# Two copies of a convolution's input and accumulator, and a new order of ScalarE's work

## The chip, the cores and the metric

The kernel runs on one core of a Trainium2 chip. The metric is the device time of one execution in microseconds (us), lower being better.

## What is computed

`x` is 8 samples of 256 tokens by 256 channels. A first layer (attention with modulated weights) adds to `x`; a second layer, a gated state-space block, adds to the result. The change lies in the first third of the second layer, cut here to what matters:

```python
xr, gate = jnp.split(x @ W_in.T, 2, axis=-1)          # 256 -> 512 + 512 channels
xr = xr + t_emb[:, None, :]
xc = conv1d(xr, W_conv, taps=4, causal, per channel) + b_conv
xc = silu(xc)
mu, var = xc.mean(-1), xc.var(-1)                     # layer norm over the 512 channels
xn = (xc - mu) / sqrt(var + 1e-5) * ln_g + ln_b
Bm, Cm, dt = split(xn @ W_xproj.T, 3)                 # 16 numbers each per token
...
_, ys = scan(step, h0, (Ad, Bd, xn, Cm))              # 256 steps in time, all samples at once
y = ys + D * xn
return y * silu(gate) @ W_out.T
```

## The kernel before, in words

The program is written out by hand, one instruction stream for each engine, with semaphores between them; within an engine the order of the code is the order of the work. There are four stages: the first layer, sample by sample (0 to 301 us of the trace); the **convolution stage**, sample by sample (301 to 385 us); a stage that normalises the rows, splits them into three bf16 parts and writes them to DRAM (385 to 464 us); the scan of 256 steps with the output projection (464 to 719 us). The stages follow one another: the statistics at L1266 to L1271 need all eight samples of the convolution stage, and everything later needs the statistics.

Samples are b = 0 to 7, channels lie on the 128 partitions in CT = 4 groups of 128. For each sample the convolution stage has these steps:

- TensorE, `project_in(b)` (L868 to L880): 8 column blocks, each of two matmuls of 256 columns. The first four blocks go to banks 4 and 5 (the convolution's input, signalled by `xr_done`), the other four to banks 6 and 7 (the gate, signalled by `gate_done`). The first half waits until ScalarE has emptied banks 4 and 5 of the sample before (`xr_in`), the second half until it has emptied banks 6 and 7 (`gate_out`). Each fp32 matmul has two records in the profile, so one sample's half is x16 and the whole is x32.
- ScalarE, `take_projection` (L569 to L587): four activations take banks 4 and 5 into the padded input `xrp` (L575), four multiply it by the last tap into the accumulator `acc` (L580, then `tap3_ready`), two take the gate through SiLU into `gateT` (L585) after a wait for `gate_done`.
- VectorE, `convolve` (L1234 to L1242): twelve multiply-adds put the other three taps onto `acc` (then `conv_done`).
- ScalarE, `gate_conv` (L596 to L601): SiLU of `acc` into `xcT` (then `xcT_ready`). `xcT` has one copy, before and after the change.
- TensorE, `to_tokens` (L912 to L928): waits for `xcT_ready`, turns `xcT` into token order with 8 transposes (L919, into banks 0 and 1), then multiplies it with the small weights `wxg` (L926, 48 columns each, into bank 2; then `xcT_used`).
- ScalarE, `take_tokens` (L589 to L594): two copies of banks 0 and 1 into `xc`.
- VectorE, `take_raw` (L1244 to L1253): a copy of bank 2 and two batch-norm statistics instructions.

The order on each engine before the change, for b from 1 to 7:

- ScalarE: `take_projection(b)`, `take_tokens(b-1)`, `gate_conv(b)`. `take_projection(b)` waits until the convolution of b-1 is done (L573), since `xrp` and `acc` have one copy each.
- VectorE: `convolve` of b, `take_raw(b-1)`.
- TensorE (L907 to L935): `project_in(b)`, `to_tokens(b-1)`, beginning with `project_in(0)` and `project_in(1)`; at the end `to_tokens(6)` and `to_tokens(7)` follow each other. In the loop a turn is thus the pair "project in b, then to tokens b-1":

```python
with pe.Fori(2, B) as b:
    project_in(b, False)
    to_tokens(b - 1, False)
to_tokens(B - 1, False)
```

GpSimd clears the three padding columns of `xrp` once (L397) and otherwise fills constants; SyncE issues no transfer in this stage.

Of the kernel before, what the change touches and what calls it, by code (L numbers as in the profile page):

```python
# [19 lines left out]
ALU = mybir.AluOpType  # L20
ACT = mybir.ActivationFunctionType
AX = mybir.AxisListType

P = 128
B, S, H = 8, 256, 256
NH, HD = 16, 16
C, NS = 512, 16
TAPS = 4
HALVES = S // P
NT = B * HALVES  # L30
HT, CT = H // P, C // P
# [50 lines left out]
def build(nc, x_tok, xT, s1_row, condT, w5T, winT, wconv, bconv, ln_row, lnT, wxT, wxdt, wdtT, bdt_row, alog_row,  # L82
          woT, ident_d, mask8_d, out):
    with ExitStack() as ctx:
        def sb(name, shape, dt=F32):
            return ctx.enter_context(nc.sbuf_tensor(name, shape, dt))

        def sem(name):
            return ctx.enter_context(nc.semaphore(name))
# [7 lines left out]
        bank = [ctx.enter_context(nc.psum_tensor(f"bank{i}", [P, 512], F32)) for i in range(8)]  # L97
# [7 lines left out]
        wcv = sb("wcv", [P, CT, TAPS])  # L105
# [92 lines left out]
        def sbc(name, shape, dt=F32):  # L198
            return conv_bufs.enter_context(nc.sbuf_tensor(name, shape, dt))

        xrp = sbc("xrp", [P, CT, TAPS - 1 + S])
        acc = sbc("acc", [P, CT, S])
        xcT = sbc("xcT", [P, CT, S])
        conv_bufs.close()
        xpart = sb1("xpart", [P, HALVES * XS, 3, C], BF16)
# [21 lines left out]
        s = {n: sem(n) for n in names}  # L227
# [5 lines left out]
        def _(sp):  # L233
# [76 lines left out]
            def store_b(t):  # L310

                for j, (_, bp) in enumerate(PAIRS):
                    rows = bd_d[j * BD_J:j * BD_J + B * (S * P + NS)].rearrange("(b q) -> b q", b=B)[:, 0:S * P]
                    rows = rows.rearrange("b (t c) -> t b c", c=P)[:, :, 0:NS]
                    sp.dma_start(rows[t * P:(t + 1) * P], bpart[:, bp, t, :].rearrange("p (b d) -> p b d", b=B))\
                      .then_inc(s[f"bd_out{t}"], 16)
# [58 lines left out]
        def _(pool):  # L375
            own = Own(pool, s["pool_own"])
# [17 lines left out]
                        .then_inc(s["part_ready"], 1)  # L394

            pool.wait_ge(s["x1_ready"], B)
            nc.gpsimd.memset(xrp[:, :, 0:TAPS - 1], 0.0).then_inc(s["const_pool"], 1)  # L397
            nc.gpsimd.memset(xst[:, :, :, :], 1.0)
            nc.gpsimd.memset(bst[:, :, :, :], 0.0)
            nc.gpsimd.memset(cst[:, :, :, :], 0.0)  # L400
# [9 lines left out]
            with pool.Fori(0, B // XS) as i:  # L410
                for k in range(XS):
                    b = i * XS + k
# [60 lines left out]
        def _(act):  # L473
# [92 lines left out]
            act.wait_ge(s["x1_ready"], B)  # L566
            nc.scalar.activation(tA[:, :], tA[:, :], ACT.Tanh).then_inc(s["dt_out"], 1)

            def take_projection(b, first):  # L569

                act.wait_ge(s["xr_done"], b * 2 + 2)
                if not first:
                    act.wait_ge(s["conv_done"], b)  # L573
                for c in range(CT):
                    ins = nc.scalar.activation(xrp[:, c, TAPS - 1:], bank[4 + c // 2][:, (c % 2) * S:(c % 2 + 1) * S],  # L575
                                               ACT.Identity, bias=cond[:, c, bass.ds(b, 1)])
                ins.then_inc(s["xr_in"], 1)
                act.wait_ge(s["xr_in"], b + 1)
                for c in range(CT):
                    ins = nc.scalar.activation(acc[:, c, :], xrp[:, c, TAPS - 1:], ACT.Identity,  # L580
                                               bias=bcv[:, c:c + 1], scale=wcv[:, c, TAPS - 1:TAPS])
                ins.then_inc(s["tap3_ready"], 1)
                act.wait_ge(s["gate_done"], b * 2 + 2)
                for c2 in range(2):
                    ins = nc.scalar.activation(gateT[:, 2 * c2:2 * c2 + 2, bass.ds(b * S, S)],  # L585
                                               bank[6 + c2][:, :].rearrange("p (k s) -> p k s", k=2), ACT.Silu)
                ins.then_inc(s["gate_out"], 1)  # L587

            def take_tokens(b):  # L589

                for t in range(HALVES):
                    act.wait_ge(s["tok_ready"], b * HALVES + (t + 1))
                    nc.scalar.activation(xc[:, b * HALVES + t, :], bank[t][:, :], ACT.Copy)\
                        .then_inc(s["tok_taken"], 1)  # L594

            def gate_conv(b, first):  # L596

                act.wait_ge(s["conv_done"], b + 1)
                if not first:
                    act.wait_ge(s["xcT_used"], b)  # L600
                nc.scalar.activation(xcT[:, :, :], acc[:, :, :], ACT.Silu).then_inc(s["xcT_ready"], 1)  # L601

            take_projection(0, True)
            gate_conv(0, True)
            with act.Fori(1, B) as b:
                take_projection(b, False)
                take_tokens(b - 1)
                gate_conv(b, False)
            take_tokens(B - 1)
            act.wait_ge(s["rt_in"], 5)  # L610
            nc.scalar.activation(rt[:, :], var_e[:, :], ACT.Sqrt).then_inc(s["rt_out"], 1)
# [459 lines left out]
        def _(dve):  # L1071
            v = nc.vector
            own = Own(dve, s["vec_own"])
# [147 lines left out]
            for c in range(CT):  # L1221
                v.tensor_scalar(wxg[:, c, :], wx[:, c, :], lnt[:, 0, c:c + 1], None, ALU.mult)
                ins = v.tensor_scalar(lnb_rep[:, c, :], ones[:, :], lnt[:, 1, c:c + 1], None, ALU.mult)
# [7 lines left out]
            sample(B - 1, False, True, False)  # L1231
            add_l0(B - 1)

            def convolve():  # L1234
                for k in range(TAPS - 1):
                    for c in range(CT):
                        ins = v.scalar_tensor_tensor(acc[:, c, :], xrp[:, c, k:k + S], wcv[:, c, k:k + 1],  # L1237
                                                     acc[:, c, :], ALU.mult, ALU.add)
                    if k < TAPS - 2:
                        own.mark(ins)  # L1240
                        own.settle()
                ins.then_inc(s["conv_done"], 1)  # L1242

            def take_raw(b):  # L1244

                dve.wait_ge(s["tok_taken"], b * HALVES + HALVES)
                dve.wait_ge(s["xcT_used"], b + 1)
                v.tensor_copy(raw[:, bass.ds(b * HALVES, HALVES), :],
                              bank[2][:, 0:2 * 64].rearrange("p (t n) -> p t n", t=HALVES)[:, :, 0:NP3])\
                    .then_inc(s["raw_ready"], 1)  # L1250
                for t in range(HALVES):
                    ins = v.bn_stats(bn[:, b * HALVES + t, :], xc[:, b * HALVES + t, :])
                own.mark(ins)  # L1253

            dve.wait_ge(s["tap3_ready"], 1)
            convolve()
            with dve.Fori(1, B) as b:
                own.enter(b - 1, TAPS - 1)
                dve.wait_ge(s["tap3_ready"], b + 1)
                convolve()  # L1260
                take_raw(b - 1)
            own.leave(B - 1)
            take_raw(B - 1)
            own.settle()
            for n in range(NT):
# [181 lines left out]
```

## Time and profile before

| | us |
|---|---|
| median of three runs | 718.82 |
| lowest and highest of them | 718.27 and 719.84 |
| span of the profiled execution (first to last instruction) | 718.9 |
| convolution stage, from the first `xrp` activation to the last copy of bank 2 | 301.4 to 385.2 |

Busy shares over the whole span: TensorE 72%, VectorE 70%, ScalarE 37%, GpSimd 18%. The page gives no time for the profiled execution beside its span, so the span stands for both. In the rows below, times are microseconds from the start of the span; a row of a timeline merges neighbouring instructions of one line (x12 is twelve of them), and what stands in square brackets is the time that the engine was idle before the row and the instruction that released it. PEclk is the clock that TensorE was granted, as a part of full speed: 1.00 is 2.4 GHz and 0.50 is 1.2 GHz. A matmul's record ends when the result is there, so matmuls that follow closely overlap in their records.

### The profile page before, as it was taken

Reading aid. Unit: us, or ns where it says so; the run is one execution under the profiler, and the core shown is the slowest. Engines: PE = TensorE matmul, PEld = TensorE weight load, DVE = VectorE, ACT = ScalarE, POOL = GpSimd, SP = SyncE. Lnnn points to the kernel's source line nnn. Section 1 sums busy time; section 2 is a strip of 40 time slices with the busy share of each in tenths; the row PEclk is TensorE's granted clock in tenths of the full one; section 3 lists DMA queues with packets and bytes.
Section 4 is the critical chain, followed back from the end, with each engine's and each line's share of the span. In section 5 each row is a group of like instructions: output and inputs, shape, how many; then the busy total and the mean of one; then the engine's idle time right before and its main releaser. Section 6 shows DMA issues by size and latency. Waiting matters only on the chain.

```text
span 718.9 us, 10868 instructions
## 1 busy us (share of the span) xinstructions
PE 515.4 (72%) x3248; PEld 302.7 (42%) x3264; DVE 500.2 (70%) x820; ACT 263.7 (37%) x513; POOL 129.9 (18%) x136
## 2 busy tenths in 40 slices
PE   3667888888888878999972100187677668888878
PEld 2555556465564634688862000011111113333357
DVE  2834858667595775467666897188898878888832
ACT  2314453445545433366673555012112112222211
POOL 5302012020120200240000246011221112222100
PEclk9868999999999998999995555589999989999999
DMA  9635161624606240040000234644454446556341
GB/s 356 216 71 103 31 129 26 113 52 80 118 16 130 51 81 1 1 175 0 0 0 1 88 117 157 77 90 86 98 98 93 92 85 128 117 115 135 84 147 51
DMA packets 44889, 64.88 MB, mean 90 GB/s; under 512 B 19536, under 2 KB 34256, under 8 KB 41152
## 3 DMA queue, kind: packets, MB, share of 16 engines
q1 hardware_dynamic: 41520, 59.26, 37.0%
q0 software_dynamic: 784, 3.15, 1.1%
q10 hardware_dynamic: 2560, 2.16, 0.9%
q8 instruction: 12, 0.20, 0.1%
q14 instruction: 13, 0.11, 0.0%
HBM read 41.88 MB, written 22.61 MB: 90 GB/s over the span
## 4 chain that ended last, share of the span: by engine, by line
PE 37%; issue 20%; DVE 19%; DMA 10%; ACT 7%; POOL 4%; SPq 2%; ACTq 0%; DVEq 0%; POOLq 0%
DVE zst L1378 15%; PE bank L718 6%; PE bank L965 6%; ACT ex L540 5%; PE bank L975 5%; PE bank L736 4%; DMA bst<-bd_d 3%; DMA qst<-mT 3%; PE bank L746 3%; PE bank L1061 2%; PE bank L773 2%; PE bank L727 2%; PE bank L756 2%; POOL xpart L416 2%; DVE mx L1175 2%
## 5 line engine op out<-in xcount | busy, mean ns | idle before, releaser
L1378 DVE CUSTOM_DVE_ANT_0 zst<-zst,bank,hi 128x512 f32<-128x512 f32 x256 | 191.3, 747 | 43.6 <-PE bank L965 22.2
L965 PE MATMUL bank<-xst,bst 128*128 128x512 bf16 x240 | 87.5, 404 | 102.5 <-DMA bst<-bd_d 57.7
L648 ACT ACTIVATE yb<-bank,ybias 128x512 f32<-128x512 f32 x64 | 44.1, 689 | 186.9 <-PE bank L975 182.4
L965 PEld LDWEIGHTS bank<-xst,bst 128*128 128x128 bf16 x256 | 24.7, 98 | 187.3 <-DVE zst L1378 120.5
L1175 DVE TENSOR_REDUCE mx<-bank 128x2 f32<-128x512 f32 x128 | 80.0, 686 | 18.1 <-PE bank L736 17.0
L540 ACT ACTIVATE ex<-bank 128x512 f32<-128x512 f32 x128 | 66.1, 609 | 41.1 <-PE bank L746 23.5
L975 PE MATMUL bank<-zst,cst 128*32 128x512 f32 x512 | 70.2, 621 | 0.9 <-DVE zst L1378 0.9
L1193 DVE TENSOR_TENSOR esum<-ex 128x1024 f32<-128x1024 f32 x32 | 39.1, 1223 | 42.7 <-ACT ex L540 42.7
L1237 DVE SCALAR_TENSOR_TENSOR acc<-xrp,wcv,acc 128x256 f32<-128x256 f32 x96 | 40.1, 481 | 29.4 <-ACT acc L580 28.8
L877 PE MATMUL bank<-xres,win 128*128 (+1 forms) x256 | 57.6, 382 | 1.2 <-ACT gateT L585 0.7
L718 PE MATMUL bank<-xnT,w 128*128 128x256 f32 x192 | 52.3, 422 | 5.1 <-ACT xnT L487 5.1
L389 POOL TENSOR_TENSOR qk<-qk,part 128x512 f32<-128x512 f32 x16 | 19.7, 1233 | 196.8 <-ACT part L502 196.7
L877 PEld LDWEIGHTS bank<-xres,win 128*128 128x128 f32 x256 | 47.9, 190 | 8.5 <-issue 1.2
L746 PE MATMUL bank<-qst,kst 97*128 97x256 bf16 x256 | 40.5, 280 | 13.0 <-DMA qst<-mT 10.2
L736 PE MATMUL bank<-kst,qst 96*128 96x256 bf16 x256 | 38.6, 286 | 8.0 <-DMA kst<-qk_d 4.8
L718 PEld LDWEIGHTS bank<-xnT,w 128*128 128x128 f32 x192 | 38.7, 212 | 12.5 <-ACT xnT L487 6.9
L416 POOL TENSOR_TENSOR xpart<-xrem,xpart 128x512 bf16<-128x512 f32 x16 | 20.7, 1311 | 109.6 <-ACT xpart L627 109.6
L423 POOL TENSOR_TENSOR cst<-cP,mask 128x64 f32<-128x64 f32 x32 | 9.6, 302 | 163.3 <-PE bank L975 163.3
L763 PE MATMUL bank<-ex,vp 128*32 128x256 f32 x512 | 33.9, 382 | 7.2 <-ACT ex L540 7.2
L746 PEld LDWEIGHTS bank<-qst,kst 97*128 97x128 bf16 x256 | 20.0, 99 | 36.2 <-ACT ex L540 20.1
L736 PEld LDWEIGHTS bank<-kst,qst 96*128 96x128 bf16 x256 | 24.1, 101 | 22.1 <-issue 8.2
L1154 DVE SCALAR_TENSOR_TENSOR xres<-bank,dc,xres 128x256 f32 (+1 forms) x32 | 14.0, 480 | 22.8 <-PE bank L781 21.9
(169 smaller groups left out, 712.3 us busy)
## 6 DMA issues: line engine op xcount, KB each, us to landing
qk_d<-part SPq DMA_DIRECT2D x64, 96.0 KB, 2.5
xs_d<-xpart SPq DMA_DIRECT2D x16, 384.0 KB, 2.6
xst<-xs_d SPq DMA_DIRECT2D x32, 192.0 KB
xst<-xs_d SPq DMA_DIRECT2D x32, 128.0 KB
y_d<-yb SPq DMA_DIRECT2D x128, 32.0 KB
ytk<-y_d SPq DMA_DIRECT2D x16, 256.0 KB, 3.6
bst<-bd_d SPq DMA_DIRECT2D x32, 102.0 KB
qst<-qk_d SPq DMA_DIRECT2D x8, 384.0 KB, 4.6
```

Of the source, the lines that this page charges most:

```text
L540: nc.scalar.activation(ex[:, g % 2, n % 4, :], bank[4 + n % 4][:, :], ACT.Exp, scale=SCALE)\
L648: nc.scalar.activation(yb[:, par, g, :], bank[4 + n % 2][:, :], ACT.Identity, bias=ybias[:, bass.ds(i * (2 * CH // 4) + n, 1)]).then_inc(s ...
L718: ins = mm(bank[bk][:, o * S:(o + 1) * S], w5[:, w, k, o * P:(o + 1) * P], xnT[:, k, :], start=k == 0, stop=k == HT - 1)
L736: ins = mm(bank[4 + n % 4][:, t * S:(t + 1) * S], qst[0:96, par, HEADS[n], t * P:(t + 1) * P], kst[0:96, par, HEADS[n], :], start=True, st ...
L746: ins = mm(bank[4 + n % 4][:, t * S:(t + 1) * S], kst[0:97, par, HEADS[n], t * P:(t + 1) * P], qst[0:97, par, HEADS[n], :], start=True, st ...
L877: ins = mm(bank[4 + c // 2][:, (c % 2) * S:(c % 2 + 1) * S], win[:, k, c * P:(c + 1) * P], xres[:, k, bass.ds(b * S, S)], start=k == 0, st ...
L965: mm(bank[k][:, :], bst[:, par, step, :], xst[:, par, step, :], start=True, stop=True)\
L975: ins = mm(bank[4 + g % 2][32 * k:32 * k + 32, :], cst[:, par, step, :], zst[:, step % ZR, :], start=True, stop=True)
L1175: v.tensor_reduce(mx[:, :, HEADS[n]:HEADS[n] + 1], bank[4 + n % 4][:, :].rearrange("p (t k) -> p t k", t=HALVES), AX.X, ALU.max)\
L1193: v.tensor_tensor(esum[:, g % 2, :, :], ex[:, g % 2, :, 0:S], ex[:, g % 2, :, S:], ALU.add)\
L1237: ins = v.scalar_tensor_tensor(acc[:, c, :], xrp[:, c, k:k + S], wcv[:, c, k:k + 1], acc[:, c, :], ALU.mult, ALU.add)
L1378: v._custom_dve(bass.dve_ops.TENSOR_ADD_SAT, out=zst[:, t % ZR, :], in0=zst[:, (t - 1) % ZR, :], in1=bank[t % 4][:, :], s0=hi[:, t:t + 1], ...
```

## The change

`xrp` and `acc` get a second copy each, used in turn by even and odd samples; the memset clears the padding of both. ScalarE's order becomes: `take_projection(0)`, `take_projection(1)`, `gate_conv(0)`, then for b = 0 to 5 `take_tokens(b)`, `take_projection(b+2)`, `gate_conv(b+1)`, and at the end `take_tokens(6)`, `gate_conv(7)`, `take_tokens(7)`. `take_projection(b)` now waits for the convolution of b-2, and for its own SiLU of b-2 ahead of the accumulator. VectorE's order of work is as before, its loop covers two samples. TensorE's code is not touched. The new buffers lie where `xpart` has its place later, so no other buffer moves.

```diff
-        xrp = sbc("xrp", [P, CT, TAPS - 1 + S])
-        acc = sbc("acc", [P, CT, S])
+        xrp = sbc("xrp", [P, 2, CT, TAPS - 1 + S])
+        acc = sbc("acc", [P, 2, CT, S])
...
-            nc.gpsimd.memset(xrp[:, :, 0:TAPS - 1], 0.0).then_inc(s["const_pool"], 1)
+            nc.gpsimd.memset(xrp[:, :, :, 0:TAPS - 1], 0.0).then_inc(s["const_pool"], 1)
...
-            def take_projection(b, first):
+            def take_projection(b, k):
 
                 act.wait_ge(s["xr_done"], b * 2 + 2)
-                if not first:
-                    act.wait_ge(s["conv_done"], b)
+                if not (isinstance(b, int) and b < 2):
+                    act.wait_ge(s["conv_done"], b - 1)
                 for c in range(CT):
-                    ins = nc.scalar.activation(xrp[:, c, TAPS - 1:], bank[4 + c // 2][:, (c % 2) * S:(c % 2 + 1) * S],
+                    ins = nc.scalar.activation(xrp[:, k, c, TAPS - 1:], bank[4 + c // 2][:, (c % 2) * S:(c % 2 + 1) * S],
                                                ACT.Identity, bias=cond[:, c, bass.ds(b, 1)])
                 ins.then_inc(s["xr_in"], 1)
                 act.wait_ge(s["xr_in"], b + 1)
+                if not (isinstance(b, int) and b < 2):
+                    act.wait_ge(s["xcT_ready"], b - 1)
                 for c in range(CT):
-                    ins = nc.scalar.activation(acc[:, c, :], xrp[:, c, TAPS - 1:], ACT.Identity,
+                    ins = nc.scalar.activation(acc[:, k, c, :], xrp[:, k, c, TAPS - 1:], ACT.Identity,
                                                bias=bcv[:, c:c + 1], scale=wcv[:, c, TAPS - 1:TAPS])
                 ins.then_inc(s["tap3_ready"], 1)
                 act.wait_ge(s["gate_done"], b * 2 + 2)
...
-            def gate_conv(b, first):
+            def gate_conv(b, k, first):
 
                 act.wait_ge(s["conv_done"], b + 1)
                 if not first:
                     act.wait_ge(s["xcT_used"], b)
-                nc.scalar.activation(xcT[:, :, :], acc[:, :, :], ACT.Silu).then_inc(s["xcT_ready"], 1)
-
-            take_projection(0, True)
-            gate_conv(0, True)
-            with act.Fori(1, B) as b:
-                take_projection(b, False)
-                take_tokens(b - 1)
-                gate_conv(b, False)
+                nc.scalar.activation(xcT[:, :, :], acc[:, k, :, :], ACT.Silu).then_inc(s["xcT_ready"], 1)
+
+            take_projection(0, 0)
+            take_projection(1, 1)
+            gate_conv(0, 0, True)
+            with act.Fori(0, B // 2 - 1) as i:
+                for k in range(2):
+                    take_tokens(i * 2 + k)
+                    take_projection(i * 2 + (k + 2), k)
+                    gate_conv(i * 2 + (k + 1), 1 - k, False)
+            take_tokens(B - 2)
+            gate_conv(B - 1, 1, False)
             take_tokens(B - 1)
...
-            def convolve():
+            def convolve(par):
                 for k in range(TAPS - 1):
                     for c in range(CT):
-                        ins = v.scalar_tensor_tensor(acc[:, c, :], xrp[:, c, k:k + S], wcv[:, c, k:k + 1],
-                                                     acc[:, c, :], ALU.mult, ALU.add)
+                        ins = v.scalar_tensor_tensor(acc[:, par, c, :], xrp[:, par, c, k:k + S], wcv[:, c, k:k + 1],
+                                                     acc[:, par, c, :], ALU.mult, ALU.add)
...
             dve.wait_ge(s["tap3_ready"], 1)
-            convolve()
-            with dve.Fori(1, B) as b:
-                own.enter(b - 1, TAPS - 1)
-                dve.wait_ge(s["tap3_ready"], b + 1)
-                convolve()
-                take_raw(b - 1)
-            own.leave(B - 1)
+            convolve(0)
+            with dve.Fori(0, B // 2 - 1) as i:
+                own.enter(i, 2 * (TAPS - 1))
+                for k in range(2):
+                    dve.wait_ge(s["tap3_ready"], i * 2 + (k + 2))
+                    convolve(1 - k)
+                    take_raw(i * 2 + k)
+            own.leave(B // 2 - 1)
+            dve.wait_ge(s["tap3_ready"], B)
+            convolve(1)
+            take_raw(B - 2)
             take_raw(B - 1)
```

## Rows read from the trace of the kernel before

**Rows 1.** Busy time by engine in the convolution stage; columns: stretch, length, engines, PEclk, DMA

```profile
301.00:385.30 84.30, 75.86 (x424) 66.51 (x422) 49.78 (x119) 55.34 (x107) 12.59 (x9) 0.95 0.09 38
```

**Rows 2.** Waits of that stage: engine, line, releaser, us, times, longest

```profile
DVE acc L1237 <- ACT acc L580: 28.8, 8, 4.7
ACT xcT L601 <- DVE acc L1237: 25.4, 8, 3.2
PEld bank L919 <- issue: 2.5, 6, 0.5
```

**Rows 3.** Timeline, ScalarE, one turn: start us, us, engine, line, operation, count, idle before

```profile
329.83 1.06 ACT L601 ACTIVATE xcT<-acc 128x1024 f32<-128x1024 f32 x1 [3.23 <-DVE acc L1237]
330.80 1.55 ACT L575 ACTIVATE xrp<-bank,cond 128x256 f32<-128x256 f32 x4
332.38 2.08 ACT L580 ACTIVATE acc<-xrp,bcv,wcv 128x256 f32<-128x256 f32 x4
334.37 1.06 ACT L585 ACTIVATE gateT<-bank 128x512 f32 x2
335.32 1.07 ACT L593 ACTIVATE xc<-bank 128x512 f32 x2
339.62 1.06 ACT L601 ACTIVATE xcT<-acc 128x1024 f32<-128x1024 f32 x1 [3.23 <-DVE acc L1237]
```

**Rows 4.** Timeline, VectorE, the same turn (12 instructions in one row)

```profile
334.50 5.09 DVE L1237 SCALAR_TENSOR_TENSOR acc<-xrp,wcv,acc 128x256 f32<-128x256 f32 x12 [3.34 <-ACT acc L580]
```

**Rows 5.** Timeline, TensorE's weight loads (PEld) and matmuls (PE), the same turn

```profile
333.63 6.78 PEld L877 LDWEIGHTS bank<-xres,win 128*128 128x128 f32 x32
340.81 0.85 PEld L919 LDWEIGHTS bank<-ident,xcT 128*128 128x128 f32 x8 [0.40 <-issue]
...
331.02 1.09 PE L919 MATMUL bank<-ident,xcT 128*128 128x128 f32 x8
333.67 7.14 PE L877 MATMUL bank<-xres,win 128*128 x32
```

**Rows 6.** Timeline, TensorE, where the stage begins

```profile
303.12 3.69 PE L877 MATMUL bank<-xres,win 128*128 128x256 f32 x16 [0.45 <-ACT xrp L575]
307.55 3.72 PE L877 MATMUL bank<-xres,win 128*128 128x256 f32 x16 [0.73 <-ACT gateT L585]
311.36 1.09 PE L919 MATMUL bank<-ident,xcT 128*128 128x128 f32 x8
```

**Rows 7.** Timeline, TensorE and then VectorE, where the stage ends

```profile
370.18 1.09 PE L919 MATMUL bank<-ident,xcT 128*128 128x128 f32 x8
371.10 1.88 PE L926 MATMUL bank<-wxg,xcT 128*128 128x48 f32 x16
379.88 1.97 PE L919 MATMUL bank<-ident,xcT 128*128 128x128 f32 x8 [6.89 <-ACT xcT L601]
381.64 3.49 PE L926 MATMUL bank<-wxg,xcT 128*128 128x48 f32 x16
...
385.24 0.26 DVE L1248 COPY raw<-bank 128x96 f32<-128x96 f32 x1 [5.14 <-PE bank L926]
```

**Rows 8.** Busy time and granted clock (PEclk) in four short stretches of the first layer

```profile
61.00:63.00 2.00, 1.86 (x18) 1.84 (x18) 0.09 (x1) 0.75 (x2) 0.00 (x0) 1.00 0.93 180
63.00:64.00 1.00, 0.36 (x3) 0.20 (x2) 0.57 (x4) 0.91 (x1) 0.00 (x0) 0.50 0.95 206
69.00:70.00 1.00, 1.00 (x5) 0.61 (x4) 0.00 (x0) 0.00 (x0) 0.00 (x0) 0.59 0.91 197
128.00:129.00 1.00, 0.35 (x4) 0.32 (x5) 0.53 (x2) 0.00 (x0) 0.00 (x0) 1.00 0.74 103
```

**Rows 9.** Timeline, TensorE, what it did in and before two of them

```profile
61.14 0.39 PE L835 MATMUL bank<-ident,mx 128*16 128x128 f32 x2 [2.00 <-DVE mx L1175]
62.19 1.17 PE L789 MATMUL bank<-wx,lnb_rep 128*128 128x48 f32 x8
...
128.65 1.05 PE L746 MATMUL bank<-qst,kst 97*128 97x256 bf16 x8 [2.29 <-DMA qst<-mT]
```

## The prediction, made blind

> **What bounds the kernel now.** I read the page first, then the busy time by stage, then the waits of the stage that the change touches, then one turn of it on each engine. The stages follow one another, so only the convolution stage counts, and its length passes straight to the end. In it TensorE is busy 75.9 of 84.3 us, VectorE 49.8, ScalarE 55.3 [rows 1]. The waits seem to ask for the change: VectorE waits 28.8 us for `acc` to be filled, ScalarE 25.4 us for the convolution, while TensorE's own wait for `xcT` is 2.5 us in six turns [rows 2].
>
> One turn says more. It is 9.79 us long (329.83 to 339.62): `xcT`, `xrp`, `acc` on ScalarE [rows 3], 5.09 us of taps on VectorE [rows 4], and `xcT` again. This ring through one `acc` sets the pace. But TensorE has almost the same turn: its loads run on until 340.41 (333.63 + 6.78) and the next one starts at 340.81, so of 9.79 us only 0.40 us is waiting [rows 5]. The two rings are 4% apart. The most that faster work on `acc` can bring is a turn of 9.39 us; how TensorE is fed decides the rest.
>
> **What the change removes.** ScalarE's wait for the convolution of the same sample, and VectorE's wait for the fill. Worth 0.40 us a turn if TensorE could run on, and at the end `to_tokens(7)` would no longer wait 6.89 us [rows 7].
>
> **What it moves.** `gate_conv(b+1)` now stands behind the whole of `take_projection(b+2)`: ten activations, the last two of which wait for `gate_done` of b+2, that is for the end of `project_in(b+2)`. TensorE's next work after that is `to_tokens(b+1)`, which waits for that very `xcT`. Before, `xcT` was made ahead of the projection's waits. So TensorE finishes a projection and then stands still until ScalarE has done the gate and the SiLU. No DMA is issued by the moved steps, no queue of SP or POOL is passed.
>
> The new turn, from one start of `to_tokens` to the next:
> - `to_tokens`: 331.02 to 333.67, 2.65 us [rows 5];
> - first half of the projection until its last result: 3.69 us [rows 6];
> - hand-over to ScalarE: 0.11 us, from the nearest row (a matmul ending at 381.64 + 3.49 = 385.13, its reader starting at 385.24) [rows 7]; bounds 0.05 and 0.15;
> - `xrp`, `acc`, `gateT`: 330.80 to 335.32, 4.52 us [rows 3]. The gate's banks are full after 2.65 + 7.14 + 0.11 = 9.90 us, ScalarE gets there after 2.65 + 3.69 + 0.11 + 3.57 = 10.02 us, so this wait is just covered; if it weren't, it would cost 0.1 us;
> - `xcT`: 1.06 us [rows 3], and 0.13 us to TensorE (330.89 to 331.02) [rows 3, 5].
>
> Sum 12.16 us, bounds 12.0 and 12.3, against 9.79: **2.37 us more a turn**. Nothing else is late: the taps begin at 10.02 and are done at 15.1 us, and are wanted at 12.16 + 10.97 = 23.1 us. The copies of tokens lie beside TensorE's work. The two more waits on ScalarE are long satisfied; the work of its own that they name hides them (if not, some 0.05 us each). The memset doubles from 12 to 24 columns, on GpSimd ahead of the first `xrp`: between nothing and 0.1 us, taken as nothing.
>
> **Start.** `project_in(1)` ends at 307.55 + 3.72 = 311.27 [rows 6]. Its gate is taken at 311.38, `xcT` of sample 0 runs from 312.33 (0.95 later, as 334.37 to 335.32 [rows 3]) to 313.39, and `to_tokens(0)` starts at 313.52 instead of 311.36 [rows 6]: 2.16 us late.
>
> **End.** `to_tokens(6)` starts at 313.52 + 6 x 12.16 = 386.48 instead of 370.18 [rows 7]. The taps of sample 7 are done at 374.32 + 10.02 + 5.09 = 389.43; `to_tokens(6)` frees `xcT` at 386.48 + 2.80 = 389.28. So `xcT` of 7 ends at 390.52, `to_tokens(7)` starts at 390.65 instead of 379.88. It took 5.25 us before, since TensorE was at 1.2 GHz after its long wait; the same work took 2.80 us at 370.18 [rows 7]. Last copy of bank 2 at 393.6 (full clock) or 396.0 (low) instead of 385.24: **8.3 or 10.8 us later**. This is what is given back of the new stalls' 16.4 us.
>
> **The clock.** Before, TensorE worked without a pause from 311 to 373 us. Now it stands 2.4 us in each of seven places (before `to_tokens` 0 to 6), and each pause is followed by 8 transposes and 16 narrow records. The nearest rows of the first layer differ. At 61.14, after 2.00 us idle, came two transposes and 16 records of 48 columns, very like this; the granted clock went from 1.00 to 0.50 at 63.0 and stayed there until about 69.8 (0.59 between 69 and 70), 6.8 us [rows 8, 9]. After 2.29 us idle ending at 128.65 it stayed at 1.00 [rows 8, 9]; there a dense projection lay just ahead. So some pauses will bring the clock down to 1.2 GHz, others not; none to seven. A fall costs at least 2.45 us (5.25 less 2.80, one `to_tokens` at the low clock) and at most half of 6.8, 3.4 us, all of it ahead of the first half's end and so on the path. I take 3.2, since part of the low time falls into the pause, and four falls of seven, nearer to the row of 61.14: 12.8 us. The last `to_tokens` is then at the low clock as before, 10.8.
>
> Sum: 718.9 + 10.8 + 12.8 = 742.5; the span is within 0.1 us of the median of the runs. I say 742 us; this case's own range is 736 to 749.
>
> The Trainium skill, page "TensorE: Matmul & The Clock Gate", section "HAM oscillation — how this bites in real kernels", tells of a kernel that waits in every tile and starts each one cold. By that rule all seven pauses would cost; it is a rival below.
>
> **Rivals.**
> 1. The clock falls in no pause, or in one. For it: the pause that ends at 128.65 brought no fall [rows 8, 9]. Against: what follows the pause here is narrow work. 718.9 + 8.3 = 727.2 to 731. Chance 0.25.
> 2. It falls in all seven: 718.9 + 10.8 + 7 x 3.2 = 752.1. For it: the row at 61.14; against: the row at 128.65. Chance 0.18. This is what the skill's rule named above would make of it.
> 3. The other side, faster. If ScalarE reached `xcT` of b+1 before TensorE finished `project_in(b+2)`, the turn would be 9.39 us, `to_tokens(6)` at 311.36 + 6 x 9.39 = 367.7, and the last sample, by `project_in(7)`'s first half at 364.1, 0.11, 3.57, 5.09, 1.06, 0.13 and 2.91, done at 377.0: 8.2 us less, 710.7. It decides once `xcT` comes less than 0.40 us after the projection's last load. The waits of rows 2 speak for it; the order of the code speaks against it, since `gateT` of b+2 stands ahead. Chance 0.04. The Trainium skill, the same page, section "Architectural detail: the array is 16× 32×32, not 1× 128×128", says that ScalarE's queue is strictly first in, first out; by it this case is out. No row here shows a ready instruction behind a waiting one.
> 4. The change does nothing that can be measured, pauses and the shorter end cancelling: 0.01.
>
> **How the numbers follow.** Forecast 0.52, rivals 0.25, 0.18, 0.04, 0.01. The range 727 to 752 leaves out the faster case and the edges of rivals 1 and 2. Faster by over 0.2% (about what a measurement here can tell from no change): 0.04; within: 0.01; slower: 0.95.
>
> **What would show it.** In the profile after: turns of 12.2 us or, where the clock fell, some 15; TensorE idle about 2.4 us before each L919, released by `xcT` (L601); ScalarE's long waits at L575 for L877, hardly any at L601; VectorE's wait for `acc` longer, not shorter; TensorE's share of the stage down from 90% to some 75%. The forecast is wrong if TensorE's idle time before L919 is near zero, if PEclk stays at 1.00 through the stage (then rival 1), or if the later stages change in length by over 1 us.

## The result, and the profile after

| | before | after |
|---|---|---|
| median | 719.33 us | 756.9 us |
| lowest and highest of four runs | 718.27 and 720.86 | 750.75 and 759.64 |
| profiled execution: span, mean granted clock | 718.9 us, 0.903 | 757.8 us, 0.863 |

The ratio is 1.0526, with a 95% interval from 1.0476 to 1.0577: the change makes the kernel 5% slower. Forecast was 742 us, with a range of 727 to 752. The time of an execution is about 1.8 us more than its span (759.64 and 757.8 us in the profiled one), so spans are compared with spans below and times with times.

The four stages after (stretch, length, busy time of TensorE matmuls, weight loads, VectorE, ScalarE and GpSimd, granted clock, DMA):

```profile
0.00:302.00 302.00, 238.84 (x1802) 161.09 (x1803) 192.13 (x328) 122.86 (x249) 46.99 (x43) 0.93 0.42 94
302.00:427.20 125.20, 105.94 (x424) 92.32 (x422) 50.35 (x118) 56.74 (x107) 12.58 (x9) 0.72 0.06 26
427.20:505.00 77.80, 2.60 (x16) 1.77 (x18) 56.09 (x101) 31.60 (x70) 23.83 (x20) 0.50 0.37 99
505.00:757.80 252.80, 198.37 (x1008) 73.62 (x1022) 203.07 (x274) 53.52 (x87) 46.48 (x65) 0.96 0.48 102
```

The convolution stage grew from 84.3 us [rows 1] to 125.2 us, by 40.9. Divided in the same way, the kernel before has 301.0 us for the first layer, 77.8 for the stage behind the convolution and 255.8 for the scan. So the first layer is 1.0 us longer, the stage behind is the same to 0.1 us, the scan is 3.0 us shorter; together 38.9, which is the difference of the spans. The scan's 3 us are within what the program does by itself: in the ten traces of this case, whose kernels are the same from there on, the part behind the last copy of bank 2 takes between 330.3 and 335.0 us, and 333.7 before and 330.6 after are both inside. So the place is the one predicted. TensorE's clock there is 0.72 after 0.95: its work is the same, but its records now last 105.9 us and not 75.9.

The waits of that stage after the change (us in total, times, longest):

```profile
DVE acc L1243 <- ACT acc L582: 54.4, 8, 8.5
ACT xrp L575 <- PE bank L883: 51.5, 6, 8.8
...
PE bank L925 <- ACT xcT L603: 17.9, 8, 2.5
```

Against [rows 2]: VectorE waits 54.4 us for `acc` where it waited 28.8, although it now has two of them. ScalarE's 25.4 us before the SiLU are gone, and 51.5 us before `xrp` have come: it waits for TensorE's projection. And TensorE waits 17.9 us in eight places for `xcT`. Reading the three together gives a ring: TensorE waits for ScalarE, ScalarE for TensorE, and VectorE stands beside it.

One turn on ScalarE, then on TensorE (start us, us, engine, line, operation, count, idle before), then VectorE's taps in that turn:

```profile
341.27 1.56 ACT L575 ACTIVATE xrp<-bank,cond 128x256 f32<-128x256 f32 x4 [8.72 <-PE bank L883]
342.87 2.07 ACT L582 ACTIVATE acc<-xrp,bcv,wcv 128x256 f32<-128x256 f32 x4
344.85 1.05 ACT L587 ACTIVATE gateT<-bank 128x512 f32 x2
345.80 1.05 ACT L603 ACTIVATE xcT<-acc 128x1024 f32<-128x1024 f32 x1
```

```profile
314.26 1.09 PE L925 MATMUL bank<-ident,xcT 128*128 128x128 f32 x8 [2.12 <-ACT xcT L603]
...
329.87 1.96 PE L925 MATMUL bank<-ident,xcT 128*128 128x128 f32 x8 [2.47 <-ACT xcT L603]
...
334.91 9.68 PE L883 MATMUL bank<-xres,win 128*128 x32
346.99 1.96 PE L925 MATMUL bank<-ident,xcT 128*128 128x128 f32 x8 [2.40 <-ACT xcT L603]
```

```profile
327.86 5.09 DVE L1243 SCALAR_TENSOR_TENSOR acc<-xrp,wcv,acc 128x256 f32<-128x256 f32 x12 [8.46 <-ACT acc L582]
```

ScalarE idles 8.72 us before `xrp`, does `xrp`, `acc`, `gateT` without a gap, and only then `xcT` at 345.80. VectorE had finished that sample's taps at 327.86 + 5.09 = 332.95, and the narrow matmuls (331.62 + 3.49) had freed the single copy of `xcT` at 335.11. So the SiLU was ready to run for 10.7 us and stood behind work whose input was not there. This is what the Trainium skill, page "TensorE: Matmul & The Clock Gate", section "Architectural detail: the array is 16× 32×32, not 1× 128×128", calls a strictly first-in, first-out queue; the trace agrees, and here are the rows that the kernel before could not give.

The turn is 346.99 - 329.87 = 17.12 us, where 12.16 had been worked out. Step by step: transposes and narrow matmuls 5.04 us (329.87 to 334.91) for 2.65; first half of the projection with the hand-over 6.36 (334.91 to 341.27) for 3.80; ScalarE to the start of `xcT` 4.53 for 4.52; `xcT` and the hand-over 1.19 for 1.19. The last two are as forecast to 0.01 us. The first two contain all of the 4.96 us that are missing, and both are TensorE's. Its granted clock in that turn:

```profile
327.50:329.87 2.37, 0.01 (x1) 0.01 (x1) 1.98 (x5) 2.23 (x4) 0.00 (x0) 0.99 0.01 3
329.87:334.91 5.04, 5.04 (x25) 5.04 (x25) 3.04 (x8) 1.19 (x2) 0.00 (x0) 0.50 0.00 0
334.91:337.50 2.59, 2.59 (x7) 2.14 (x8) 1.45 (x3) 0.00 (x0) 0.00 (x0) 0.50 0.00 0
337.50:341.20 3.70, 3.70 (x13) 2.99 (x13) 0.00 (x0) 0.00 (x0) 0.00 (x0) 0.66 0.00 0
341.20:344.60 3.40, 3.39 (x16) 2.65 (x14) 0.00 (x0) 3.29 (x8) 0.00 (x0) 1.00 0.00 0
```

TensorE is granted 2.4 GHz during the pause, to within its last 0.05 us, and 1.2 GHz from the first transpose on. The 0.66 of the fourth row means low until about 340.0 (a share x at 0.5 and the rest at 1.0 gives x = 0.68). So it was low for 10.2 us, and then high for 6.9 us, until the next transposes, which last 1.96 us again. From 329.87 to 415.36 there are five such turns, of 17.0 to 17.2 us.

The end of the stage:

```profile
415.36 1.97 PE L925 MATMUL bank<-ident,xcT 128*128 128x128 f32 x8 [2.40 <-ACT xcT L603]
...
421.81 1.97 PE L925 MATMUL bank<-ident,xcT 128*128 128x128 f32 x8 [1.21 <-ACT xcT L603]
...
427.17 0.26 DVE L1254 COPY raw<-bank 128x96 f32<-128x96 f32 x1 [5.01 <-PE bank L932]
```

### The profile page after: what moved, and what is told of

It is laid out like the page before. It is cut to its first block, busy times and chain, and to the rows that moved or that the text cites. A ratio compares the mean times of both kernels' runs of the same rounds, so it can differ in the third digit from the quotient of the medians.

```text
span 757.8 us, 10837 instructions
## 1 busy us (share of the span) xinstructions
PE 545.8 (72%) x3248; PEld 328.8 (43%) x3264; DVE 501.6 (66%) x820; ACT 264.7 (35%) x513; POOL 129.9 (17%) x136
## 4 chain that ended last, share of the span: by engine, by line
PE 35%; issue 26%; DVE 17%; DMA 8%; ACT 6%; POOL 5%; SPq 2%; ACTq 0%; POOLq 0%; DVEq 0%
DVE zst L1388 13%; PE bank L971 6%; PE bank L724 5%; PE bank L981 5%; ACT ex L540 5%; PE bank L742 4%; DMA bst<-bd_d 3%; PE bank L752 3%; DMA qst<-mT 3%; PE bank L779 2%; PE bank L733 2%; PE bank L1067 2%; PE bank L762 2%; DVE mx L1181 2%; POOL xpart L416 2%
## 5 line engine op out<-in xcount | busy, mean ns | idle before, releaser
L1243 DVE SCALAR_TENSOR_TENSOR acc<-xrp,wcv,acc 128x256 f32<-128x256 f32 x96 | 40.1, 481 | 55.0 <-ACT acc L582 54.4
L883 PE MATMUL bank<-xres,win 128*128 (+1 forms) x256 | 72.7, 453 | 1.2 <-ACT gateT L587 0.7
L883 PEld LDWEIGHTS bank<-xres,win 128*128 128x128 f32 x256 | 59.0, 234 | 12.7 <-issue 1.2
L724 PE MATMUL bank<-xnT,w 128*128 128x256 f32 x192 | 50.0, 408 | 5.0 <-ACT xnT L487 5.0
L575 ACT ACTIVATE xrp<-bank,cond 128x256 f32<-128x256 f32 x32 | 12.5, 476 | 51.5 <-PE bank L883 51.5
```

The lines of the kernel that those rows point to most:

```text
L724: ins = mm(bank[bk][:, o * S:(o + 1) * S], w5[:, w, k, o * P:(o + 1) * P], xnT[:, k, :], start=k == 0, stop=k == HT - 1)
L883: ins = mm(bank[4 + c // 2][:, (c % 2) * S:(c % 2 + 1) * S], win[:, k, c * P:(c + 1) * P], xres[:, k, bass.ds(b * S, S)], start=k == 0, st ...
L1243: ins = v.scalar_tensor_tensor(acc[:, par, c, :], xrp[:, par, c, k:k + S], wcv[:, c, k:k + 1], acc[:, par, c, :], ALU.mult, ALU.add)
```

## The experiments

**The order of ScalarE's work, or the copies?** First the changed kernel with the SiLU put ahead of the next projection:

```diff
                 for k in range(2):
                     take_tokens(i * 2 + k)
+                    gate_conv(i * 2 + (k + 1), 1 - k, False)
                     take_projection(i * 2 + (k + 2), k)
-                    gate_conv(i * 2 + (k + 1), 1 - k, False)
```

> Both copies and VectorE's loop as after the change; only ScalarE's order inside a turn differs: the tokens of b, the SiLU of b+1, then the whole projection of b+2. Theory (the SiLU stands behind the gate's wait, TensorE pauses, its clock falls): the pauses before the transposes shrink to 0.4 us, PEclk stays at 1.00 until the end of the stage, the turn is again set by the ring taps 5.09 + SiLU 1.06 + fill 3.57 = 9.8 us, and the time is 716 to 722 us. Rival (the second copies themselves, or VectorE's new loop, cost the time): still over 745 us.

Measured: 718.9 us, ratio 1.0003 (0.9974 to 1.0032). TensorE's first turn and the next, and two SiLUs on ScalarE:

```profile
312.79 1.88 PE L925 MATMUL bank<-ident,xcT 128*128 128x128 f32 x8 [2.12 <-ACT xcT L603]
...
327.40 1.04 PE L925 MATMUL bank<-ident,xcT 128*128 128x128 f32 x8
...
336.97 1.04 PE L925 MATMUL bank<-ident,xcT 128*128 128x128 f32 x8
...
342.94 1.06 ACT L603 ACTIVATE xcT<-acc 128x1024 f32<-128x1024 f32 x1 [3.30 <-DVE acc L1243]
...
352.73 1.06 ACT L603 ACTIVATE xcT<-acc 128x1024 f32<-128x1024 f32 x1 [3.23 <-DVE acc L1243]
```

Two adjacent calls exchanged take back the whole loss. Inside the loop no pause is left after the first one. That one comes from the start of the stage, where `take_projection(1)` still stands ahead of the first SiLU: TensorE is idle 2.12 us, its clock falls, and this turn takes 14.6 us (312.79 to 327.40). I had expected 1.00 throughout; the fall happened in the profiled run, whose time, 725.4 us, is the longest of the ten. The later turns on TensorE are 9.57 us (327.40 to 336.97), not the 9.8 of the ring over `acc`. The ring is still there: ScalarE's SiLUs follow each other by 9.78 to 9.86 us. TensorE was behind them after its slow first turn and caught up by some 0.2 us in each of the later ones, so 9.57 us is what its own work takes (see below), and not a new bound of this kernel.

Then the copies alone, with ScalarE in the old order:

```diff
             take_projection(0, 0)
-            take_projection(1, 1)
             gate_conv(0, 0, True)
+            take_projection(1, 1)
+            take_tokens(0)
+            gate_conv(1, 1, False)
             with act.Fori(0, B // 2 - 1) as i:
                 for k in range(2):
-                    take_tokens(i * 2 + k)
                     take_projection(i * 2 + (k + 2), k)
-                    gate_conv(i * 2 + (k + 1), 1 - k, False)
-            take_tokens(B - 2)
-            gate_conv(B - 1, 1, False)
+                    take_tokens(i * 2 + (k + 1))
+                    gate_conv(i * 2 + (k + 2), k, False)
             take_tokens(B - 1)
```

> Both copies, the doubled memset and VectorE's loop as after the change, with ScalarE's order as before it. Theory (the order costs, the copies do nothing by themselves, since each SiLU still stands ahead of the next fill): turns of 9.8 us set by the ring over acc, 718 to 721 us. Rival (the copies let the ring open by themselves): 9.4 us a turn, 716 us or less.

Measured: 718.64 us beside 718.09, ratio 1.0006 (0.9978 to 1.0035). The turn is 9.78 us, as before the change:

```profile
329.31 1.09 PE L925 MATMUL bank<-ident,xcT 128*128 128x128 f32 x8
...
339.09 1.09 PE L925 MATMUL bank<-ident,xcT 128*128 128x128 f32 x8
```

The second copies, the larger memset and VectorE's new loop cost nothing and bring nothing while the SiLU of a sample stands ahead of the next fill.

**The pause and the clock taken apart.** The changed kernel with dense work in the pause:

```diff
+            def fill(n):
+
+                for _ in range(n):
+                    mm(bank[3][:, 0:S], win[:, 0, 0:P], xres[:, 0, 0:S], start=True, stop=True)
+
             project_in(1, False)
+            fill(5)
             to_tokens(0, True)
             with pe.Fori(2, B) as b:
                 project_in(b, False)
+                fill(5)
                 to_tokens(b - 1, False)
```

> The changed kernel with five more matmuls of 256 columns (ten records, some 2.2 us) on TensorE between each projection and the transposes, written to an unused bank; they leave the result as it is and lie in the pause. Theory (pause and clock are two costs): PEclk stays at 1.00, turns of 12.2 us as first worked out, and about 727 us. Rival (the lengthening comes from the order alone, the low clock merely goes with it): no gain, 750 us or more. Rival (the filler delays the transposes and so adds its own time): 727 plus up to 7 x 2.2 us, 742 us.

Measured: 730.99 us, ratio 1.0169 (1.0118 to 1.0219). The filler (L939), the next two transposes, the last sample's, and the clock over the whole loop:

```profile
335.66 2.32 PE L939 MATMUL bank<-xres,win 128*128 128x256 f32 x10
338.23 1.09 PE L925 MATMUL bank<-ident,xcT 128*128 128x128 f32 x8 [0.25 <-ACT xcT L603]
...
350.49 1.09 PE L925 MATMUL bank<-ident,xcT 128*128 128x128 f32 x8 [0.32 <-ACT xcT L603]
...
391.35 1.78 PE L925 MATMUL bank<-ident,xcT 128*128 128x128 f32 x8 [1.42 <-ACT xcT L603]
...
313.78:387.13 73.35, 71.66 (x398) 63.08 (x397) 38.21 (x90) 39.83 (x78) 0.37 (x1) 1.00 0.11 43
```

With a filler that computes nothing of use the kernel is some 26 us faster than without it (756.9 - 731.0). The pause has shrunk to 0.25 and 0.32 us, but the turns are 12.2 us (338.23 to 350.49: 12.26), the 12.16 that had been worked out: the filler only took the place of the idling. The clock is 1.00 through the loop. So of 37.6 us (756.9 - 719.3) by the medians, 11.7 are the pauses less what the end gives back, and about 26 are the clock. The traces agree on the first and give more for the second: from the first `xrp` activation to the last copy of bank 2 this kernel takes 94.70 us, the changed one 124.86 and the kernel before 83.81, so 10.9 us are the pauses and 30.2 the clock; the profiled execution of the changed kernel is the longest of its four. Forecast were 10.8 and 12.8. The 727 us expected for this run had the last `to_tokens` at full clock; it came mostly at the low one, after a pause of 1.42 us that stands right behind `to_tokens(6)`.

**How long a pause does the clock bear?** Two doses. First the gate's activations behind the SiLU, which shortens the pause to 1.5 us:

```diff
                 ins.then_inc(s["tap3_ready"], 1)
+
+            def take_gate(b):
+
                 act.wait_ge(s["gate_done"], b * 2 + 2)
...
                     take_projection(i * 2 + (k + 2), k)
                     gate_conv(i * 2 + (k + 1), 1 - k, False)
+                    take_gate(i * 2 + (k + 2))
```

> As the changed kernel, but the two gate activations and their wait stand behind the SiLU of b+1. Theory: the pause shrinks by the gate's 0.95 us to about 1.5 us, the turn at full clock is 11.2 us, 718.9 + 7 x 1.4 less what the end gives back, about 723 us if the clock stays, and 740 or more if it falls at each pause as well; this run tells how long a pause the clock bears here. Rival (the wait on the gate's banks is what counts, not the place of the SiLU): about 719 us.

Measured: 725.12 us, ratio 1.0109 (1.0052 to 1.0165). Two us over the 723 worked out for a clock that stays. Turns of 11.2 to 11.3 us, pauses of 1.44 to 1.51 us, and a clock of 1.00 in the loop:

```profile
334.24 1.09 PE L931 MATMUL bank<-ident,xcT 128*128 128x128 f32 x8 [1.44 <-ACT xcT L606]
...
345.53 1.09 PE L931 MATMUL bank<-ident,xcT 128*128 128x128 f32 x8 [1.51 <-ACT xcT L606]
...
311.71:379.28 67.57, 58.72 (x337) 51.69 (x337) 38.37 (x91) 39.54 (x79) 1.65 (x3) 1.00 0.12 47
```

So the place of the SiLU counts, not the wait for the gate's banks alone, and these pauses of 1.5 us cost only themselves. Second, one filler matmul in place of five (`fill` as above), which leaves pauses of 2.0 us:

```diff
...
             project_in(1, False)
+            fill(1)
             to_tokens(0, True)
             with pe.Fori(2, B) as b:
                 project_in(b, False)
+                fill(1)
                 to_tokens(b - 1, False)
```

> The changed kernel with a single more matmul (two records, 0.44 us) ahead of the wait, which leaves a pause of 2.0 us between the 1.5 us that the clock bore and the 2.4 us at which it fell each time. Theory (how often it falls depends on the pause's length): falls in some turns, 735 to 752 us. Rival (it falls at each pause of 2 us as at 2.4): 757 us. Other rival (one matmul is enough): 731 us.

Measured: 742.41 us, ratio 1.0323 (1.026 to 1.0386). The transposes of four turns, and the stretches in which the clock fell and rose in the third:

```profile
314.82 1.09 PE L925 MATMUL bank<-ident,xcT 128*128 128x128 f32 x8 [1.69 <-ACT xcT L603]
...
330.42 1.09 PE L925 MATMUL bank<-ident,xcT 128*128 128x128 f32 x8 [2.04 <-ACT xcT L603]
...
342.61 1.09 PE L925 MATMUL bank<-ident,xcT 128*128 128x128 f32 x8 [1.97 <-ACT xcT L603]
...
358.19 1.09 PE L925 MATMUL bank<-ident,xcT 128*128 128x128 f32 x8 [2.04 <-ACT xcT L603]
...
343.00:344.00 1.00, 1.00 (x12) 1.00 (x10) 0.98 (x3) 0.61 (x2) 0.00 (x0) 0.93 0.00 0
350.00:351.00 1.00, 1.00 (x4) 0.83 (x3) 0.00 (x0) 0.00 (x0) 0.00 (x0) 0.65 0.00 0
```

The turns alternate: 15.60 us, 12.19, 15.58 (342.61 to 358.19) and so on, with the fall in four of the seven. In the third the clock falls in the narrow matmuls, at about 343.9, and is back at about 350.7: 6.8 us low, and 3.4 us lost, as long as the low stretch of the first layer [rows 8]. This kernel behaves as my forecast said that the changed one would, and takes the 742 us that I had forecast for that one. It also shows that neither the pause nor the work behind it decides alone: the work is the same in every turn, the clock held after 2.04 us and fell after 1.97, and in the first turn it fell after 1.69.

**Is it the pause, or what stands behind it?** The pause left as it is, and dense work put between it and the transposes, on the path:

```diff
                 pe.wait_ge(s["xcT_ready"], b + 1)
+                for _ in range(5):
+                    mm(bank[3][:, 0:S], win[:, 0, 0:P], xres[:, 0, 0:S], start=True, stop=True)
```

> The changed kernel with five more matmuls of 256 columns (2.2 us) after TensorE's wait for xcT and ahead of the transposes, so on the path: the pause of 2.4 us stays, and dense work follows it. Theory (the clock fell because narrow work follows the pause): it falls in few turns or none; turns of 12.2 + 2.2 = 14.4 us, about 746 us, so faster than the changed kernel although it does more. Rival (the pause alone brings the clock down, each time): turns of 19 us or more, above 775 us.

Measured: 746.39 us beside 718.09, ratio 1.04 (1.0315 to 1.0484); the changed kernel's ratio is 1.0526. The filler (L922) of three turns, and the stretches in which the clock fell and rose:

```profile
326.80 2.43 PE L922 MATMUL bank<-xres,win 128*128 128x256 f32 x10 [2.39 <-ACT xcT L603]
...
341.11 3.75 PE L922 MATMUL bank<-xres,win 128*128 128x256 f32 x10 [2.32 <-ACT xcT L603]
...
357.18 2.43 PE L922 MATMUL bank<-xres,win 128*128 128x256 f32 x10 [2.39 <-ACT xcT L603]
...
342.00:343.00 1.00, 1.00 (x5) 0.78 (x4) 0.96 (x3) 0.00 (x0) 0.00 (x0) 0.53 0.00 0
345.00:346.00 1.00, 1.00 (x10) 1.00 (x8) 0.00 (x0) 0.22 (x1) 0.00 (x0) 0.77 0.00 0
```

The pauses are 2.32 and 2.39 us, within 0.1 us of those in the changed kernel, and each turn has 2.2 us more work on the path, yet the kernel is faster. The intervals of the two ratios just touch; the two traces differ more clearly, with 112.75 us for the stage where the changed kernel takes 124.86. A turn is 14.31 us where the clock stays (326.80 to 341.11) and 16.07 us where it falls (341.11 to 357.18). It fell in two of the seven turns, for about 3.4 us each time (from about 342.1 to 345.5). The pause alone doesn't bring the clock down each time. With narrow work behind, pauses of 2.1 to 2.5 us did so in all nine places where they occur: seven in the changed kernel, the first turn of the kernel with the SiLU first, and the end of the one with the gate last (384.46, after 2.38 us). That the narrow work is the reason is not shown: the filler also makes the turn another length, and the kernel before has a counterexample in its first layer, shown further below.

**An order that beats both kernels.** The SiLU between the two halves of the fill, ahead of everything that waits for the second half of the projection (`take_input` ends with the `xrp` activations, `take_rest` has `acc` and the gate):

```diff
                 ins.then_inc(s["xr_in"], 1)
+
+            def take_rest(b, k):
+
                 act.wait_ge(s["xr_in"], b + 1)
...
                     take_tokens(i * 2 + k)
-                    take_projection(i * 2 + (k + 2), k)
+                    take_input(i * 2 + (k + 2), k)
                     gate_conv(i * 2 + (k + 1), 1 - k, False)
+                    take_rest(i * 2 + (k + 2), k)
```

> As the changed kernel, but the SiLU of b+1 stands between the xrp and the acc activations of b+2, so that it waits for nothing but the first half of the projection. Theory: TensorE never waits for it, PEclk 1.00 through the loop, turns of 9.4 us set by TensorE alone; the last SiLU waits for the last taps, so the last transposes start some 5 us earlier than before the change: 711 to 715 us, faster than both kernels. Rival (the ring over acc is the bound whatever the order): turns of 9.8 us and 718 to 720 us.

Measured: 715.17 us, ratio 0.9961 (0.9935 to 0.9987). One turn on ScalarE and TensorE, and the last sample's transposes:

```profile
325.71 1.57 ACT L575 ACTIVATE xrp<-bank,cond 128x256 f32<-128x256 f32 x4 [3.09 <-PE bank L889]
327.15 1.07 ACT L606 ACTIVATE xcT<-acc 128x1024 f32<-128x1024 f32 x1
...
328.86 1.04 PE L931 MATMUL bank<-ident,xcT 128*128 128x128 f32 x8
...
338.43 1.04 PE L931 MATMUL bank<-ident,xcT 128*128 128x128 f32 x8
...
374.71 1.97 PE L931 MATMUL bank<-ident,xcT 128*128 128x128 f32 x8 [4.82 <-ACT xcT L606]
```

TensorE no longer waits in the loop, and is now its bound: turns of 9.57 us (328.86 to 338.43), not the 9.4 that I had expected. The last transposes start at 374.71, and still at 1.2 GHz after a pause of 4.82 us. In this trace the stage itself begins 1.69 us earlier than in the kernel before (first `xrp` at 299.74 and 301.43), so of the 5.17 us to the 379.88 of [rows 7] only 3.5 are the order's doing; the stage is 3.5 us shorter as a whole, and the median 4.1. So the same kernel with nine filler matmuls there:

```diff
                 to_tokens(b - 1, False)
+            for _ in range(9):
+                mm(bank[3][:, 0:S], win[:, 0, 0:P], xres[:, 0, 0:S], start=True, stop=True)
             to_tokens(B - 1, False)
```

> As the kernel with the SiLU between the two halves of the fill, with nine more matmuls (some 3.9 us) into an unused bank between the last two samples' transposes, where TensorE stood 4.8 us. Theory (the low clock there costs half of the last transposes and narrow matmuls, 2.45 us): PEclk 1.00 at the last samples' transposes, 712.7 us. Rival (no effect on the end, since the last taps decide): 715.2 us.

Measured: 712.23 us beside 718.09, ratio 0.992 (0.9888 to 0.9953). The filler runs from 371.16 for 4.12 us, then come the last transposes and narrow matmuls:

```profile
376.14 1.10 PE L931 MATMUL bank<-ident,xcT 128*128 128x128 f32 x8 [0.86 <-ACT xcT L606]
377.08 1.88 PE L938 MATMUL bank<-wxg,xcT 128*128 128x48 f32 x16
```

They take 376.14 to 378.96, 2.82 us, where they took 5.25. This is the fastest of the kernels run, 0.8% below the kernel before.

All kernels side by side; the stage is taken from the start of the first `xrp` activation to the start of the last copy of bank 2 in the profiled execution:

| kernel | median, us | stage, us | against before |
|---|---|---|---|
| before | 718.1 to 719.3 | 83.81 | |
| changed | 756.9 | 124.86 | +41.05 |
| SiLU first | 718.9 | 87.79 | +3.98 |
| copies alone | 718.64 | 83.75 | -0.06 |
| five fillers in the pause | 730.99 | 94.70 | +10.89 |
| gate last | 725.12 | 88.72 | +4.91 |
| one filler in the pause | 742.41 | 106.74 | +22.93 |
| five fillers behind the pause | 746.39 | 112.75 | +28.94 |
| SiLU between the halves | 715.17 | 80.33 | -3.48 |
| the same, nine fillers at the end | 712.23 | 77.90 | -5.91 |

## Why the prediction was wrong, point by point

- **Direction and place: right.** Slower, in the convolution stage alone, by a pause of TensorE before `to_tokens` that comes from the SiLU standing behind the next sample's gate. Exchanging two calls (718.9 us) and running the copies alone (718.6) show both halves of this. Rival 3, faster through a turn of 9.39 us, needed the SiLU ahead of that wait; a kernel with such an order exists among the experiments, not in the change. It gained 3.5 us of stage, not the 8.2 of the rival's sum, since the turn is 9.57 us and the last `to_tokens` stays at the low clock. (By its own terms that sum should also have the first half of `project_in(7)` end at 358.31 + 2.65 + 3.69 = 364.65, not 364.1, and so give 7.7.)
- **The turn at full clock, 12.16 us: right.** 12.2 us with the clock held. The pauses in the changed kernel's turns are 2.40 and 2.47 us for a forecast of 2.4, and the start (`to_tokens(0)` 11.95 us after the first `xrp` activation, forecast 12.09) fits too. The sum without falls was 10.8 us and came out as 10.9 in the trace with the filler, 11.7 by the medians.
- **"Four falls of seven": wrong, it was all seven** in the profiled execution. The first layer had two rows, one with a fall and one without, and I took a number between them. They are not alike: behind the pause at 61.14 came narrow records, as in the changed kernel, behind the one at 128.65 dense ones; the row at 61.14 taken alone would have given seven. Rival 2 had the count right. But what stands behind the pause is not the whole rule: the same trace has a third such pause, which I had not used, and there the clock fell with dense work behind:

```profile
268.04 3.60 PE L736 MATMUL bank<-kst,qst 96*128 96x256 bf16 x12 [2.39 <-DVE mx L1175]
...
267.00:268.00 1.00, 0.00 (x0) 0.00 (x0) 1.00 (x3) 0.00 (x0) 0.00 (x0) 0.90 0.00 0
...
274.00:275.00 1.00, 1.00 (x6) 0.72 (x5) 0.00 (x0) 0.00 (x0) 0.00 (x0) 0.69 0.00 0
```

After 2.39 us idle it was low from about 267.8 to 274.6, 6.8 us. So two of the first layer's three pauses of 2.0 to 2.4 us brought a fall, which speaks for more falls than the four that I took.

- **"A fall costs 3.2 us, at most 3.4": wrong, this is the term that was mis-sized.** I had bounded the cost by half of the 6.8 us that the first layer stayed low. In the changed kernel it stayed low for 10.2 us. A turn with such a fall is 17.12 us, 4.96 more than one without. The first one (314.26 to 329.87) was low for 6.8 us and cost 3.45, and the last, at `to_tokens(6)`, 2.3, since no projection follows it: 6.45 us from 415.36 to 421.81 for the 4.17 in my working. Sum 3.45 + 5 x 4.94 + 2.3 = 30.4 us in the profiled run, for a forecast of 12.8; the difference of the two traces, with the filler and without, is 30.2. With seven falls at 3.2 us I had 752.1 for rival 2. With the measured costs the stage grows by 10.8 + 30.4 = 41.2 us, and it did by 41.05.
- **"Half of the low time": right by itself,** since nearly all of it lies on the path: 4.96 of 10.2 us. The upper bound failed because it took the length of one low stretch in another stage for the longest there can be. That the 5 us of narrow work at the low clock ahead of the dense part (5.25 us in [rows 7]) made the stretch longer is my reading, not shown.
- **The range** (727 to 752) reached to the middle of rival 2, without its upper side. The measured median lies 4.9 us above it. One of the four runs, at 750.75, lies within; falls may have been fewer in it, but only the run of 759.64 has a trace.
- **The page's rule** from the Trainium skill, "TensorE: Matmul & The Clock Gate", section "HAM oscillation — how this bites in real kernels", that a kernel which waits in each tile can start each one cold: the trace agrees, with low work from 329.87, and again in each turn up to 415.36. It described this kernel better than my mean of two rows, though the waits that it tells of are for transfers and longer, 3 to 5 us, where these are 2.4.
- **TensorE's own turn, taken as 9.39 us: wrong by 0.18.** I had read 0.40 us of idle time between the last load of the projection and the next transposes as waiting. Without any wait the turn is 9.57 us, so only 0.22 of it was. This made the possible gain look larger than it was: 0.22 us a turn, not 0.40.

In short, the step that failed is the clock's term: four falls at 3.2 us, 12.8 us, where the traces show seven falls worth 30 us. That order and pause are the cause of the loss, and how it divides between pause and clock, is shown. Open is what decides whether the clock falls at a given pause, and whether it is then low for 3.4, 6.8 or 10.2 us. In three kernels the low stretches go with less, more and most narrow work behind the fall, but no run varied that alone; the low stretch of the kernel with the SiLU first, which begins with the first transposes (312.9 to 323.2), is 10.2 us as well, and the one at 267.8 is 6.8 us with dense work behind.

## What to carry to other kernels

A second buffer removes a wait only if the instruction it frees comes up in its engine's order; before adding one, list for each engine what stands ahead of the step that another engine waits for, and put it ahead of everything that waits for later work. When an edit puts a pause into TensorE's loop, cost the pause and the clock apart, and take the clock's price from the case whose work behind the pause is alike, counting that work at the low clock. A fall seen once can come back in every turn (seven of seven here), in every second one or in two of seven, so keep the count for all turns inside the range. A few useless dense matmuls in the pause show in one run how much of a loss is the clock.

## What the runs showed of the hardware that was not expected

- The fall of the clock repeated in every turn of the loop, with the same timing: low for 10.2 us, high for 6.9, five turns within 0.1 us of 17.1. With pauses 0.4 us shorter it repeated in every second turn, and with pauses of 1.5 us never in the loop. A short pause is no safety by itself: it fell after 1.69 us in the first turn with one filler, and at the end of the kernel with five, after 1.42 us with only transposes and narrow matmuls ahead of it.
- More work on the critical path made the kernel faster (2.2 us of dense matmuls in each turn, ratio 1.04 for 1.0526), because the granted clock stayed up longer: 0.96 from the first filler to the one ahead of `to_tokens(6)` (312.41 to 401.87), for 0.71 in the changed kernel (314.26 to 415.36).
- Pauses of 2.1 to 2.5 us were borne five times of seven with dense work behind them, and in none of seven with transposes and 48-column matmuls there. With pauses of 1.97 to 2.04 us and the same work behind each, the clock fell at three of six.
